# A score bias copied into its PSUM bank by ScalarE, and the last normalization on GpSimd from slot 56 on, in a fused sparse-attention and feed-forward kernel

## What is computed

```
queries = (query @ Wq + bq).reshape(B, L, H, E)           # H = 16 heads, E = 32
keys_flat = k @ Wk + bk;  values = keys_flat @ Wv + bv    # 32 patterns
A = sparsemax(scale * einsum('blhe,bshe->bhls', queries, keys))
x = layernorm(x + (A @ values) @ Wo + bo)
s = x @ Win + bin_
h = relu(s[..., None] * W1 + b1);  g = einsum('btmh,mh->btm', h, W2) + b2
out = layernorm(x + g @ Wout + bout)
```

## Time and profile before

| what | value |
|---|---|
| median of 3 runs | 1285.32 us (1284.85 to 4392.77) |
| the profiled execution | 1285.09 us, its span 1283.3 us |
| PE (matmul) | 1220.5 us busy, 95% |
| DVE | 1145.9 us, 89% |
| ACT | 1066.9 us, 83% |
| POOL | 708.8 us, 55% |
| granted TensorE clock, mean | 0.983 |
| DMA | 318 MB, 248 GB/s mean |

### The profile page before, as it was taken

One profiled execution on the slowest core, in us unless ns is written; L12 is line 12 of the kernel. 1 busy time (PEld: TensorE's weight loads), 2 busy tenths in 40 slices (PEclk: granted clock), 3 DMA queues, 4 the chain that ended last, 5 costly groups with the idle time before them and its releaser, 6 DMA issues. The chain is left out here.

```text
span 1283.3 us, 25185 instructions
## 1 busy us (share of the span) xinstructions
PE 1220.5 (95%) x6012; PEld 883.1 (69%) x6012; DVE 1145.9 (89%) x4538; ACT 1066.9 (83%) x2285; POOL 708.8 (55%) x1285
## 2 busy tenths in 40 slices
PE   9973899999999999999999999999999999989995
PEld 5651666677777777777777777777777777755662
DVE  4987789999999999999999999999999999967776
ACT  3661765679999999999999999999999999987786
POOL 1431345556777766666656666666566656642344
PEclk9995999999999999999999999999999999999998
DMA  6480797877988888787887877888878778678964
GB/s 208 130 222 10 198 277 247 255 221 232 313 295 284 291 313 295 259 279 261 266 278 257 274 265 260 274 262 271 264 261 284 259 264 270 198 231 280 302 198 106
DMA packets 99090, 318.10 MB, mean 248 GB/s; under 512 B 16835, under 2 KB 16835, under 8 KB 82534
## 3 DMA queue, kind: packets, MB, share of 16 engines
q1 hardware_dynamic: 98774, 316.03, 76.6%
q10 hardware_dynamic: 144, 0.26, 0.1%
HBM read 249.13 MB, written 67.11 MB: 246 GB/s over the span
## 5 line engine op out<-in xcount | busy, mean ns | idle before, releaser
L868 PE MATMUL bank<-G_sb,pT 128*128 128x512 f32 x696 | 320.1, 593 | 0.7 <-ACT pT L1096 0.7
L1490 DVE MAX8 top<-bank 128x8 f32<-128x32 f32 x2048 | 211.4, 175 | 0.0
L861 PE MATMUL bank<-A_hi,xT_lo 128*128 128x512 f32 x512 | 202.9, 396 | 0.0
L859 PE MATMUL bank<-A_hi,xT_hi 128*128 128x512 f32 x512 | 202.9, 396 | 0.0
L860 PE MATMUL bank<-A_lo,xT_hi 128*128 128x512 f32 x512 | 202.7, 396 | 0.0
L1540 DVE SCALAR_TENSOR_TENSOR acc<-hinge,w2c,acc 128x512 f32<-128x512 f32 x210 | 156.9, 747 | 47.8 <-ACT hinge L1135 47.2
L868 PEld LDWEIGHTS bank<-G_sb,pT 128*128 128x128 f32 x696 | 122.3, 190 | 106.3 <-issue 105.2
L1135 ACT ACTIVATE hinge<-s_sb,b1c,w1c 128x512 f32<-128x512 f32 x240 | 192.9, 806 | 0.0
L1106 ACT ACTIVATE unread<-y_sb,minus_means 128x512 bf16<-128x512 f32 x244 | 174.9, 717 | 12.3 <-POOL minus_means L626 11.5
L626 POOL TENSOR_TENSOR minus_means<-sums,per_row 128x1 f32<-128x1 f32 x244 | 86.2, 358 | 161.7 <-DVE y_sb L1383 161.7
L1383 DVE SCALAR_TENSOR_TENSOR y_sb<-bank,y_sb 128x512 f32<-128x512 f32 x244 | 159.6, 658 | 0.0
(11 more groups left out here) (171 smaller groups left out, 2918.2 us busy)
## 6 DMA issues: line engine op xcount, KB each, us to landing
G_sb<-G_of_heads SPq DMA_DIRECT2D x74, 1536.0 KB, 7.8
G_sb<-G_of_heads SPq DMA_DIRECT2D x38, 1024.0 KB, 6.8
x_sb<-in_L_attn_query_dram SPq DMA_DIRECT2D x128, 256.0 KB, 6.6
y_sb<-in_L_attn_query_dram SPq DMA_DIRECT2D x256, 128.0 KB, 7.1
out_dram<-o_sb SPq DMA_DIRECT2D x230, 128.0 KB, 6.5
G_sb<-G_of_heads SPq DMA_DIRECT2D x16, 1280.0 KB, 7.7
G_of_heads<-y_sb SPq DMA_DIRECT2D x64, 256.0 KB, 4.0
G_of_heads<-G_sb SPq DMA_DIRECT2D x16, 512.0 KB, 3.4
```

Source lines behind the costliest of these rows:

```text
L859: nc.tensor.matmul(ps[:], hi[:, c, :], w_hi[:, c, :], start=start and c == 0, stop=False)
L861: mm = nc.tensor.matmul(ps[:], lo[:, c, :], w_hi[:, c, :], start=False, stop=(c == C - 1))
L868: mm = nc.tensor.matmul(o[:], p_blocks[:, block_of(i, c), i % HPC, :], G_of(i, c, "raw").bitcast(F32), start=(c == plain[0]), stop=(not in ...
L1490: mx = nc.vector.max(top8[:, h, :], z_ps[i % 2][:, h * S:(h + 1) * S])
```

## The change

The product with `pick_c` and `bias_rows` (line 957) goes, with the two constants and what filled them. Instead c is put once into all rows of both score banks by a float32 product with a row of ones, and ScalarE copies one of them into SBUF as `c_rows`. The first two tiles add to what stands in the banks. For every later tile ScalarE copies `c_rows` into the bank, behind the signs and positive parts of the tile two before (126 copies of 128x512), and TensorE waits for that copy (`s_zc`) instead of `s_u1`; none of the 12 products has `start=True` any longer. The last normalization of tiles 20 to 94 (slots 56 to 130) leaves ScalarE for GpSimd, where it is the last thing in a slot. Tiles 0 to 19 stay with ScalarE, the rest with VectorE.

```diff
+        c_rows = sb("c_rows", [P, D])
+        def pool_finishes(turn, j):
+            return turn * UNROLL + j >= LAG_WO + 2 * UNROLL + 1 and not vector_finishes(turn, j)
...
@@ GpSimd
-            nc.gpsimd.memset(bias_rows[:].bitcast(F32), 0.0).then_inc(s_const, 1)
-            nc.gpsimd.memset(pick_c[:].bitcast(F32), 0.0).then_inc(s_const, 1)
...
                     fold(s_side, base + i + 1, side, s_foldc)
                     fold(s_above, base + i + 1, above, s_folds)
+                if in_range(turn, j, LAG_FINAL) and pool_finishes(turn, j):
+                    i = base + j - LAG_FINAL
+                    pool.wait_ge(s_final, i)
+                    pool.wait_ge(s_shift, norms_to(1, i))
+                    pool.wait_ge(s_store[i % OR], 32 * (i // OR))
+                    nc.gpsimd.tensor_scalar(o_sb[:, i % OR, :], y_sb[:, i % YR, :], col(rstds, 1, i),
+                                            col(shifts, 1, i), ALU.mult, ALU.add).then_inc(s_final, 1)
...
@@ TensorE
+            pe.wait_ge(s_keysTc, C)
+            pe.wait_ge(s_cc, 1)
+            for z in z_ps:
+                mm = nc.tensor.matmul(z[:], ones_row, c_full, start=True, stop=True)
+            mm.then_inc(s_czps, 1)
...
-                    if not isinstance(turn, int) or base + i >= 2:
-                        pe.wait_ge(s_u1, base + i - 1)
+                    if base + i == 1:
+                        pe.wait_ge(s_crows, 1)
+                    if base + i >= 2:
+                        pe.wait_ge(s_zc, base + i - 1)
                     z = z_ps[i % 2]
-                    nc.tensor.matmul(z[:], pick_c[:], bias_rows[:], start=True, stop=False)
-                    three_pass(z, xT_hi, xT_lo, A_hi, A_lo, start=False, first=base + i == 0).then_inc(s_score, 1)
+                    three_pass(z, xT_hi, xT_lo, A_hi, A_lo, first=base + i == 0).then_inc(s_score, 1)
...
@@ ScalarE
+            act.wait_ge(s_czps, 1)
+            nc.scalar.copy(c_rows[:], z_ps[1][:]).then_inc(s_crows, 1)
...
-                if in_range(turn, j, LAG_FINAL) and not vector_finishes(turn, j):
+                if in_range(turn, j, LAG_FINAL) and not vector_finishes(turn, j) and not pool_finishes(turn, j):
...
                     nc.scalar.activation(above[:], u_raw[:, i % 2, :], ACT.Relu, scale=2.0).then_inc(s_above, 1)
+                    if base + i + 2 < TILES:
+                        if base + i == 0:
+                            act.wait_ge(s_crows, 1)
+                        nc.scalar.copy(z_ps[i % 2][:], c_rows[:]).then_inc(s_zc, 1)
...
@@ VectorE
-            nc.vector.tensor_copy(bias_rows[0:1, :], c_full).then_inc(s_c, 1)
-            nc.vector.tensor_tensor(bias_rows[E:E + 1, :], c_full, bias_rows[0:1, :].bitcast(F32),
-                                    ALU.subtract).then_inc(s_c, 1)
```

More of the change, by code:

```diff
@@ L148, in build_kernel @@
         G_dram = nc.dram_tensor("G_of_heads", [H, P, len(G_COLS) * D], F32, kind="Internal").ap()
-        bias_rows = sb("bias_rows", [P, D], F32R)
-        pick_c = sb("pick_c", [P, P], F32R)
+        c_rows = sb("c_rows", [P, D])
         bo_row = both[0:1, :]
@@ L238, in build_kernel @@
             sem("s_WqT"), sem("s_WqTa"), sem("s_WqTv"), sem("s_cmm"), sem("s_cc"), sem("s_A"), sem("s_Ahi"))
+        s_czps, s_crows, s_zc = sem("s_czps"), sem("s_crows"), sem("s_zc")
         s_zero, s_blk, s_c = sem("s_zero"), sem("s_blk"), sem("s_c")
@@ L464, in build_kernel @@
         IDLE_PASSES = (2, 3)
-        FILLS = 10 + S
-        CONSTS = FILLS + 4
+        FILLS = 8 + S
+        CONSTS = FILLS + 2
         @block.sync
@@ L614, in _ @@
             nc.gpsimd.memset(go_on[:, :, 0:1], 0.0).then_inc(s_const, 1)
-            for n, row in enumerate((0, E)):
-                pool.wait_ge(s_const, FILLS + 2 + n)
-                nc.gpsimd.memset(pick_c[row:row + 1, :].bitcast(F32), 1.0).then_inc(s_const, 1)
             pool.wait_ge(s_wload, 16 * WLOADS)
@@ L852, in _, with three_pass @@
                 mm.then_inc(s_A, 1)
-            def three_pass(ps, hi, lo, w_hi, w_lo, start, first):
+            pe.wait_ge(s_keysTc, C)
[3 more added lines that the diff above has]
+            mm.then_inc(s_czps, 1)
+            def three_pass(ps, hi, lo, w_hi, w_lo, first):
                 for c in range(C):
@@ L858, in three_pass @@
                         pe.wait_ge(s_ready, c + 1)
-                    nc.tensor.matmul(ps[:], hi[:, c, :], w_hi[:, c, :], start=start and c == 0, stop=False)
-                    nc.tensor.matmul(ps[:], hi[:, c, :], w_lo[:, c, :], start=False, stop=False)
-                    mm = nc.tensor.matmul(ps[:], lo[:, c, :], w_hi[:, c, :], start=False, stop=(c == C - 1))
+                    nc.tensor.matmul(ps[:], hi[:, c, :], w_hi[:, c, :], start=False, stop=False, skip_group_check=True)
+                    nc.tensor.matmul(ps[:], hi[:, c, :], w_lo[:, c, :], start=False, stop=False, skip_group_check=True)
+                    mm = nc.tensor.matmul(ps[:], lo[:, c, :], w_hi[:, c, :], start=False, stop=(c == C - 1), skip_group_check=True)
                 return mm
@@ L914, in feed_forward @@
                         pe.wait_ge(s_ready, C + 2)
-                        pe.wait_ge(s_c, 5)
+                        pe.wait_ge(s_c, 3)
                 if LAST - 2 * GROUP + 2 <= base + i < ENDING[0]:
@@ L949, in slot @@
                     i = j - LAG_SCORE
-                    if base + i == 0:
-                        pe.wait_ge(s_c, 2)
                     pe.wait_ge(s_xhi, base + i + 1)
                     pe.wait_ge(s_xlo, base + i + 1)
-                    if not isinstance(turn, int) or base + i >= 2:
-                        pe.wait_ge(s_u1, base + i - 1)
+                    if base + i == 1:
+                        pe.wait_ge(s_crows, 1)
+                    if base + i >= 2:
+                        pe.wait_ge(s_zc, base + i - 1)
                     z = z_ps[i % 2]
-                    nc.tensor.matmul(z[:], pick_c[:], bias_rows[:], start=True, stop=False)
-                    three_pass(z, xT_hi, xT_lo, A_hi, A_lo, start=False, first=base + i == 0).then_inc(s_score, 1)
+                    three_pass(z, xT_hi, xT_lo, A_hi, A_lo, first=base + i == 0).then_inc(s_score, 1)
                 lead = j - LAG_CHECK
@@ L1113, in copy_s @@
                     act.wait_ge(s_ready, C + 2)
-                    act.wait_ge(s_c, 5)
+                    act.wait_ge(s_c, 3)
                 if i >= 2 * GROUP:
@@ L1331, in _ @@
             weights(2)
-            dve.wait_ge(s_cc, 1)
-            nc.vector.tensor_copy(bias_rows[0:1, :], c_full).then_inc(s_c, 1)
             rest_of_x(0)
-            dve.wait_ge(s_c, 1)
-            nc.vector.tensor_tensor(bias_rows[E:E + 1, :], c_full, bias_rows[0:1, :].bitcast(F32),
-                                    ALU.subtract).then_inc(s_c, 1)
             for c in range(C):
@@ L1474, in slot @@
                                             ALU.subtract).then_inc(s_ready, 1)
-                    dve.wait_ge(s_c, 3)
+                    dve.wait_ge(s_c, 1)
                     nc.vector.tensor_copy(Wout_lo[M:M + 1, :], rounded.bitcast(F32)).then_inc(s_c, 1)
```

## The result

The changed kernel takes 1268.48 us in the median of 4 runs (1267.38 to 1269.26); the kernel before, on the same chip, takes 1285.32. That leaves out one of its four executions, which took 4392.77 us. The ratio is 0.987 with a 95% interval of 0.9858 to 0.9882: 1.3% less, 17 us, where 1267 us were forecast. In a later series the ratio was 0.9864 (0.9848 to 0.9881).

A forecast was written before the change was run, and what follows sets the result against it. TensorE was taken as the bound from 300.94 to 1095.66 us, busy for 794.5 of 794.7. Against 1285.1 us, 0.3 + 0 - 3.0 + 0.7 - 15.3 - 0.5 = -17.8 gave 1267.3, stated as 1267 us; range 1260 to 1281.

The forecast's parts named there:

- Preparation, +0.3 us: Ahead of the first tile: two added float32 products start the first score product up to 0.9 us later; 0.3 charged.
- Tiles 0 to 21, 0: First 22 products: the copy has no cover, 0 to 2 us lost, other slots gain 0.23 us; taken as 0.
- Tiles 22 to 35, -3.0: Stage from 180.32 to 300.94 us: 15 products gone save 3.5 us at most; 3.0 taken.
- Tiles 36 to 55, +0.7: Stage from 300.94 to 481.78 us: ScalarE becomes the bound, between 4.6 us gained and 2.8 lost; 0.7 lost taken.
- The long stage, -15.3: From 481.78 to 1095.66 us: 70 products at 0.23 us save 16.1 at most, less 0.8 for VectorE's collisions.
- The last three products, -0.5: The last three score products, each without its bias product, save 0.5 us together.
- The copy, 0.51 us, ending 2 us ahead: ScalarE's copy costs 0.51 us; past 481.78 us it ends 2 us and more ahead of the score product.
- GpSimd beside the MAX8 group: Long stage: GpSimd's 0.77 us normalization just fits inside VectorE's MAX8 group, except in one slot of four.
- Rival B: Long stage: GpSimd's normalization stops VectorE in every slot, at the full 0.77 us giving 1306 us; chance 0.08.
- C: First stage and slots 36 to 55: the copy takes 0.8 us or more on the path, 1280 us; chance 0.12.
- D: Long stages: the 0.23 us return as a wait for `xT_lo` or ScalarE's copy, 1281 to 1287 us; chance 0.08.
- A2: All stages: ScalarE's waits shrink with TensorE's slot and all bounds are gained, -24.4, 1260.7 us; chance 0.08.

The follow-up runs named there:

- the early copy: The changed kernel with ScalarE's copy of the bias row moved ahead of the positive parts; 1266.82 us, ratio 0.9851.
- again: The changed kernel run and profiled once more, unaltered; 1267.54 us, ratio 0.9864.
- copy alone: The changed kernel with ScalarE keeping every last normalization it had before, the bias row still copied by ScalarE; 1285.2 us, ratio 0.9996.
- normalization ahead: The changed kernel with GpSimd's last normalization placed ahead of the two folds instead of behind them; 1269.47 us, ratio 0.9871.
- normalization twice: The changed kernel with GpSimd making the last normalization twice in a row, behind the folds; 1293.55 us, ratio 1.0064.
- the doubled product: The kernel before with the product of the bias row issued twice for each tile; 1311.89 us, ratio 1.02.
- the normalization alone: The kernel before with GpSimd making the last normalization from slot 56 on, the bias row still a TensorE product; 1285.76 us, ratio 1.0.

## Why the prediction held, step by step

The sum forecast -17.8 us. By stage the first profile of the changed kernel has +1.9 - 0.8 - 2.9 + 0.6 - 14.0 - 1.5 = -16.7, the second +1.7 - 1.2 - 2.8 - 0.9 - 14.7 + 0.2 = -17.7. The mechanism that carries the sum, one product less in a stage bound by TensorE, with both loads hidden, was right. Part of the closeness is luck: the preparation and the long stage together fell short of the forecast by 2.9 and 2.0 us, and the other stages gave back 1.8 and 1.9 us that the sum did not have.

- *Preparation, +0.3 us: mis-sized.* The first real score product starts at 21.66 us and at 21.50 in the second profile, 1.7 to 1.9 us later. The two seed products are not two instructions on the chip but four:

```profile
19.34 1.98 PE L862 MATMUL bank<-hinge,second 1*128 1x512 f32 x4
...
21.25 0.66 PE L808 MATMUL bank<-ident,x_sb 128*128 128x128 f32 x4
```

  They take 1.98 us with no wait ahead of the product. I charged a third of the 0.9 us that I had allowed, for loads that should have covered it; nothing covers it. The two VectorE instructions taken away gave nothing back.
- *Tiles 0 to 21, 0: about right.* -0.8 and -1.2 us. Cover and cost are as described at the earlier trace rows: the product waits for the copy up to 0.5 us and starts about where it did. The gain of 2 us that stands open there is what the early copy shows. What the stage did gain lies in the slot of the sort and the next one: tiles 0 to 11 take 68.9 us (69.0 before), these two slots 43.4 instead of 45.2, and the rest of the stage 1.0 us more. I had not expected this, and no run explains it.
- *Tiles 22 to 35, -3.0: right,* -2.9 and -2.8 us. I spoke of 15 and 70 products in two stages, since a row counts the product on the boundary in both; the stages hold 14 and 69, whose bounds are 3.2 and 15.9 us. That moves the sum by 0.2.
- *Tiles 36 to 55, +0.7: right in kind.* +0.6 and -0.9 us; over the five profiles with the same code there (changed, again, copy alone, normalization ahead, normalization twice) -0.9 to +0.6, most near -0.6. ScalarE is busy for 174.3 us, where 175.5 were worked out. That its waits for shifts are fixed was wrong by half: the 8.1 us of the earlier trace rows are 4.0 in the changed kernel, and copy alone shows them shrink in the long stage. That ScalarE alone is the bound was incomplete. With its load taken off, VectorE and GpSimd hold the stage as long.
- *The long stage, -15.3: right, a little high.* -14.0 and -14.7 us. The mean distance is 599.83 / 69 = 8.69 us, inside the 8.66 to 8.70 named. TensorE's listed waits in it:

```profile
PE bank L975 <- DVE differs L1417: 1.1, 2, 0.8
PE bank L899 <- ACT s_sb L1129: 0.5, 1, 0.5
```

  The floor by the doubled product is 598.2, so 1.0 to 1.6 us are left to waits, where 0.8 was charged.
- *The last three products, -0.5: right.* The two distances between the last three products are 0.37 us shorter in every kernel without the bias product. What stands behind the last product takes 168.3 to 171.0 us over the kernels of the table, the doubled normalization aside, and decides the column "rest" more than they do.
- *The copy, 0.51 us, ending 2 us ahead: right.* Median 587 ns, 0.52 us start to start at 694.26, its end at 694.87 and the product at 697.57: 2.7 us of cover. The lower bound, a copy out of PSUM, was the value. The Trainium skill's ScalarE: Activation LUTs (Step-by-step: what each stage is for) says that for an ACTIVATE PSUM is the destination of lower latency than SBUF. This trace agrees as far as it can be read: the copy from SBUF into PSUM takes 0.59 us, and line 1161's copy of 512 columns from SBUF into SBUF, on 64 partitions, 0.62 us.
- *GpSimd beside the MAX8 group: right.* In the changed kernel:

```profile
694.95 1.65 DVE L1501 MAX8 top<-bank 128x8 f32<-128x32 f32 x16
...
695.79 0.77 POOL L737 TENSOR_SCALAR o_sb<-y_sb,rstds,shifts 128x512 f32<-128x512 f32 x1
...
696.63 0.42 DVE L1518 TENSOR_TENSOR_SCAN cum<-go_on,top 128x128 f32<-128x128 f32 x1
...
706.19 0.87 POOL L737 TENSOR_SCALAR o_sb<-y_sb,rstds,shifts 128x512 f32<-128x512 f32 x1
...
706.48 0.86 DVE L1547 TENSOR_SCALAR acc<-hinge,w2c,b2c 128x512 f32<-128x512 f32 x1
```

  In this slot it ends at 696.56, 0.07 us ahead of the scan. In 51 of the 69 slots it lies beside the MAX8 group alone; in 17, one in four, it collides, as at 706.19, where `acc` of line 1547 takes 0.86 us (0.52 on the mean before). VectorE's busy time in the stage even falls, from 584.2 to 577.7 us. GpSimd's line 688 (689 before) comes earlier and leaves `u_sb` alone; it meets the small `step` instead, which costs 7.9 us more in all. Of the 69 `u_sb` in the long stage, before and after:

```profile
L1461 DVE SCALAR_TENSOR_TENSOR u_sb<-step,u_raw 128x512 f32<-128x512 f32 x69 | 63.3, 917 | 2.4
```

```profile
L1472 DVE SCALAR_TENSOR_TENSOR u_sb<-step,u_raw 128x512 f32<-128x512 f32 x69 | 48.0, 696 | 2.4
```

  The mean falls from 0.92 to 0.70 us. With the normalization alone `u_sb` falls as well, to 48.2 us, and VectorE's busy time still rises by 10 us. There the fit did not hold: in 28 of 69 slots the scan starts while the normalization runs, and it takes 0.66 us on the mean instead of 0.42. It mostly ends 0.27 us behind the normalization's end, so it stands until that is done. TensorE was the bound there and the 10 us cost nothing. So the 0.05 us were as thin as feared. What I had not seen is that there is a second free place, beside `xT_lo`.
- *Rival B* priced 0.43 us a slot as break-even. Doubled, the normalization costs 0.32 us a slot and the kernel is 0.6% slower than before: its mechanism is real, its condition was not met. The Trainium skill's GPSIMD Engine Reference (§8, Key points) names VectorE's instructions with two SBUF inputs or in a two-port mode. These traces agree for instructions with two SBUF inputs: `u_sb`, the scan and the hinge sums of line 1551 stand in contention, the MAX8 group and `xT_lo`, which read PSUM, do not. The small `twice` of line 1427 and the `acc` of line 1547 have one SBUF tensor as input and stand in contention too; whether they run in a two-port mode no trace shows.
- *Rivals C and D* fall. C asked for a copy of 0.8 us, and a first stage longer by over 2 us. D asked for the 0.23 us to come back as a wait in the long stages, and TensorE's listed waits in the longest sum to 1.6 us. A2, which asked for all waits to give way in tiles 36 to 55, falls as well.

## What to carry to other kernels

Here ScalarE's work was 7% below TensorE's in the long stage (572.5 of 613.9 us). Work moved from TensorE to ScalarE was worth nothing until ScalarE was relieved as well, and the relief alone was worth nothing either. Where two engines stand as close, price both halves by a third run, the two together. For a GpSimd instruction look not for idle time of GpSimd but for the VectorE instructions that it will lie beside: next to those that read PSUM it was free, next to those with two SBUF operands one or both engines got slower. Where TensorE was the bound, a matmul cost its start-to-start distance, and a small float32 product must be counted by the instructions that it becomes.

## What the hardware showed that I had not expected

- A float32 product of 1x128 by 1x512 appears as two matmuls; two such products take 1.98 us, where a float32r product of 128x128 by 128x512 has its successor 0.23 us later.
- In the changed kernel's slot at 693 us the small instructions of one engine wait for the wide ones of the other:

```profile
693.04 0.19 POOL L625 TENSOR_TENSOR minus_means<-sums,per_row 128x1 f32<-128x1 f32 x1 [1.32 <-DVE y_sb L1394]
...
693.74 0.69 DVE L1472 SCALAR_TENSOR_TENSOR u_sb<-step,u_raw 128x512 f32<-128x512 f32 x1
693.76 0.72 POOL L625 TENSOR_TENSOR minus_means<-sums,per_row 128x1 f32<-128x1 f32 x1 [0.53 <-DVE y_sb L1394]
```

  GpSimd's 128x1 sum takes 0.19 us alone and 0.72 us beside VectorE's `u_sb`; it then ends within 0.05 us of that instruction's end. It works in the other direction too: VectorE's `twice`, 128x16, takes 0.16 us alone and 0.55 to 0.72 beside GpSimd's 64x512 sum.
- A wait of ScalarE that looks like a fixed latency (squares, GpSimd, shifts) shrank from 28.9 to 7.6 us in the long stage when ScalarE had no time left, in the kernel with the copy alone.
